# A scan kernel on one core: the residual add of each unit moves from VectorE to TensorE and ScalarE, and unit 0 and the end are reordered

## The reference

```python
h = table_slice[x]                                   # a gather, (2, 2048, 64)
# mixer on layernorm(h):
r = x_in = layernorm(h)
proj = layernorm(x_in, g, b) @ in_w.T                # -> conv input, gate
act = silu(dwconv(conv_input))
for way in (forward, backward):                      # mamba: conv, silu, dt, B, C
    state = state * exp(dt * A) + (dt * u) * B       # scan over 2048 tokens, 128 channels x 16 states
    y = sum_n(state * C) + u * D
    out_way = (y * silu(z)) @ out_w_way.T
h = h + (concat(fwd, bwd) * silu(gate)) @ out_w.T + r
# then a top-1 mixture of 32 small experts on layernorm(h), added to h
```

## Time and profile before

| what | value |
|---|---|
| median of 3 runs | 562.32 us (561.82 to 569.52) |
| the profiled execution's own time | 559.91 us |
| its span in the profile | 558.1 us |
| DVE busy | 489.1 us (88%) |
| POOL busy | 474.9 us (85%) |
| PE busy | 457.3 us (82%) |
| ACT busy | 372.6 us (67%) |
| chain that ended last, by engine | DVE 45%, PE 24%, issue 11%, ACT 9%, POOL 6% |

### The profile page before, as it was taken

One profiled execution on the slowest core, in us unless ns is written; L12 is line 12 of the kernel. 1 busy time (PEld: TensorE's weight loads), 2 busy tenths in 40 slices (PEclk: granted clock), 3 DMA queues, 4 the chain that ended last, 5 costly groups with the idle time before them and its releaser, 6 DMA issues.

```text
span 558.1 us, 5617 instructions
## 1 busy us (share of the span) xinstructions
PE 457.3 (82%) x1621; PEld 175.5 (31%) x1621; DVE 489.1 (88%) x606; ACT 372.6 (67%) x651; POOL 474.9 (85%) x157
## 2 busy tenths in 40 slices
PE   2976977868889797979798889888988895785877
PEld 1422422313233231424232423232324232332243
DVE  3575895989899999999999899999998999999940
ACT  2488485686877776776968497869684974564433
POOL 5552877998989989899999999999999999989700
PEclk9998998999989897989999799999997997697998
DMA  4249397949293855738493949493939392900000
GB/s 58 18 63 218 77 218 149 217 114 207 76 199 88 182 124 134 173 87 175 115 181 117 200 115 190 119 197 105 201 109 208 98 208 86 222 13 1 5 5 19
DMA packets 51008, 71.05 MB, mean 127 GB/s; under 512 B 16498, under 2 KB 17442, under 8 KB 50978
## 3 DMA queue, kind: packets, MB, share of 16 engines
q1 hardware_dynamic: 47986, 69.36, 55.0%
q0 software_dynamic: 1024, 1.05, 2.4%
q10 hardware_dynamic: 1968, 0.29, 0.3%
HBM read 60.19 MB, written 10.49 MB: 127 GB/s over the span
## 4 chain that ended last, share of the span: by engine, by line
DVE 45%; PE 24%; issue 11%; ACT 9%; POOL 6%; DMA 3%; SPq 2%; POOLq 0%; DVEq 0%; ACTq 0%
DVE st L1504 26%; DVE st L1489 8%; POOL st L491 4%; PE ps L727 3%; ACT ps L1081 2%; PE ps L628 2%; PE ps L690 2%; PE ps L703 2%; PE ps L817 2%; PE ps L715 2%; DVE zr L1510 1%; PE ps L801 1%; ACT L979 1%; PE ps L698 1%; DVE ga L1516 1%
## 5 line engine op out<-in xcount | busy, mean ns | idle before, releaser
L491 POOL TENSOR_TENSOR st<-st,repC 128x2048 f32<-128x2048 f32 x63 | 285.2, 4530 | 18.1 <-ACT carry L1087 13.0
L1504 DVE TENSOR_TENSOR_SCAN st<-ps,carry,st 128x512 f32<-128x512 f32 x192 | 235.5, 1268 | 3.7 <-ACT ps L1081 3.1
L1081 ACT ACTIVATE ps<-dtS,negA 128x512 f32<-128x512 f32 x256 | 171.2, 682 | 63.1 <-DVE st L1504 61.8
L482 POOL TENSOR_TENSOR st<-duS,repB 128x2048 f32<-128x2048 f32 x30 | 135.9, 4530 | 1.7 <-issue 1.7
L1504 DVE TENSOR_TENSOR_SCAN st<-ps,zero,st 128x512 f32<-128x512 f32 x64 | 78.9, 1270 | 1.4 <-ACT ps L1081 1.0
L715 PE MATMUL ps<-st,fold 128*32 128x512 f32 x504 | 69.0, 620 | 12.8 <-POOL st L491 12.8
L1489 DVE TENSOR_TENSOR st<-duS,ps 128x2048 f32<-128x2048 f32 x33 | 75.0, 2272 | 1.9 <-PE ps L690 1.7
L628 PE MATMUL ps<-act,wT 128*128 128x512 f32 x128 | 57.8, 593 | 0.3 <-ACT act L1025 0.3
L463 POOL DMA_INDIRECT x<-in_L_tok_ple_table,idx x32 | 31.1, 973 | 29.6 <-DMA dtS<-dt_dram 13.4
L690 PE MATMUL ps<-xr,Bw 128*128 128x512 f32 x68 | 38.2, 645 | 6.2 <-ACT bc_sb L1073 6.2
L667 PE MATMUL ps<-xr,wT 128*32 128x512 f32 x32 | 18.1, 649 | 26.3 <-DVE st L1489 26.3
(11 more groups left out here) (138 smaller groups left out, 622.2 us busy)
## 6 DMA issues: line engine op xcount, KB each, us to landing
repC<-bc_dram SPq DMA_DIRECT2D x64, 256.0 KB, 10.5
duS<-du_dram SPq DMA_DIRECT2D x60, 256.0 KB, 4.7
dtS<-dt_dram SPq DMA_DIRECT2D x60, 256.0 KB, 7.8
repB<-bc_dram SPq DMA_DIRECT2D x60, 128.0 KB, 2.9
dt_dram<-dt SPq DMA_DIRECT2D x16, 256.0 KB, 3.0
du_dram<-du SPq DMA_DIRECT2D x16, 256.0 KB, 2.0
bc_dram<-bc_sb SPq DMA_DIRECT2D x16, 64.0 KB, 11.1
dtS<-dt_dram SPq DMA_DIRECT2D x8, 128.0 KB, 3.4
```

The costliest lines, as they stand in the source:

```text
L482: pool.tensor_tensor(st[:, r], duS[:, u % 2], row, ALU.mult).then_inc(sem("dbu_pool"), 1)
L491: pool.tensor_tensor(st[:, r], st[:, r], row, ALU.mult).then_inc(sem("hc_ready"), 1)
L1081: sc.activation(decay_bank(u, r, q), dtS[:, u % 2, q], ACT.Exp, scale=negA[:, way(u), q, r:r + 1]).then_inc(sem("decay_ready"), 1)
L1504: dve.tensor_tensor_scan(st[:, r, q, order], decay_bank(u, r, q)[:, order], st[:, r, q, order], first, ALU.mult, ALU.add).then_inc(sem("sc ...
```

## The change

It has five parts.

1. For units 0 to 14 `partial` first multiplies the identity by `x0` (256 columns, start) and then adds its four products, so that PSUM holds the new h. A new `new_x` on ScalarE, at p = 10 of the next unit, copies it back to `x0` and increments `x0_added`. `add_partial` of these units leaves VectorE's p = 7. Unit 15 keeps `add_partial`.
2. VectorE's two copies of constants (L1661, L1662) move from p = 4 of unit 0 to before the first scan.
3. In unit 0 GpSimd runs `dt_times_x(1)` ahead of `by_c(0, 0)`, the last four gathers behind `by_c(0, 2)`, and `dt_times_x(2)` in unit 1 behind `by_c(0, 3)`. SyncE issues `load_B(1)` ahead of `store_dt(1)`. ScalarE's `dt_out(u)` also waits for `du_ready`.
4. TensorE runs `turn_chunk(3)` behind `skip_product(0)` and `add_nought(3)`.
5. At the end TensorE runs `logits(before)` ahead of the third of the last four `sum_states` products, all four `hidden(before, k)` ahead of `turn_normed(last)`, and one new `add_nought` ahead of `logits(last)`. ScalarE's order follows. VectorE runs `by_gate(last)` ahead of `choice(before)`.

```diff
             store_bc(1)
+            load_B(1)
             store_dt(1)
             store_du(1)
             load_du(1)
-            load_B(1)
...
+                if u == 1:
+                    dt_times_x(2)
                 if u == 0:
                     pool.wait_ge(sem("dt_first_1"), 64)
                     for t in range(TB + 4, TB + 12):
                         gather(t)
+                    dt_times_x(1)
                 if 2 in on_pool(u):
                     input_product(u, 2)
                 by_c(u, 0)
-                if u == 0:
-                    dt_times_x(1)
-                    for t in range(TB + 12, TILES):
-                        gather(t)
                 by_c(u, 1)
                 if u + 1 < UNITS:
                     input_product(u + 1, 0)
                 by_c(u, 2)
-                if u + 2 < UNITS:
+                if u == 0:
+                    for t in range(TB + 12, TILES):
+                        gather(t)
+                if 0 < u < UNITS - 2:
                     dt_times_x(u + 2)
...
+                if u + 1 < UNITS:
+
+                    pe.wait_ge(sem("u_added"), CB * batch(u) + (CB if way(u) else chunk(u) + 1))
+                    if way(u):
+                        pe.wait_ge(sem("x0_added"), u)
+                    pe.matmul(ps[:, SHORT, 0:TC * DM], ident[:], x0_of(tile0(u)).rearrange("p t d -> p (t d)"),
+                              start=True, stop=False, skip_group_check=True)
                 for t in range(TC):
                     mm = pe.matmul(ps[:, SHORT, t * DM:t * DM + DM], ga[:, t * P:t * P + P],
-                                   wT[:, 14, DM * way(u):DM * way(u) + DM], start=True, stop=True)
+                                   wT[:, 14, DM * way(u):DM * way(u) + DM], start=(u + 1 == UNITS), stop=True,
+                                   skip_group_check=True)
...
-            turn_chunk(3)
             skip_product(0)
             add_nought(3)
+            turn_chunk(3)
...
             for q in range(NQ):
+                if q == 2:
+                    logits(before)
                 if q < NQ - 1:
                     pe.wait_ge(sem("hc_ready"), NR * UNITS + q)
                 else:
-                    logits(before)
                     pe.wait_ge(sem("hc_dve"), 1)
...
             hidden(before, 2)
+            hidden(before, 3)
             turn_normed(last)
-            hidden(before, 3)
+            add_nought(1, start=True)
             logits(last)
...
             def dt_out(u):
                 sc.wait_ge(sem("dt_ps"), u)
                 wait(sc, "dt_in_dram", 16 * u)
+                sc.wait_ge(sem("du_ready"), u)
...
+            def new_x(u):
+
+                sc.wait_ge(sem("attn_ps"), u + 1)
+                sc.activation(x0_of(tile0(u)), ps[:, SHORT, 0:TC * DM].rearrange("p (t d) -> p t d", d=DM), ACT.Copy) \
+                  .then_inc(sem("x0_added"), 1)
...
                 if p == 10:
+                    if is_unit(u - 1):
+                        new_x(u - 1)
...
             hidden_relu(before, 2)
+            hidden_relu(before, 3)
             normed_out(last)
-            hidden_relu(before, 3)
...
             rates(1)
+            dve.wait_ge(sem("consts"), 1)
+            ch.mark(dve.tensor_copy(rank[:], ranki[:]))
+            ch.mark(dve.tensor_copy(w1[DM:DM + E], maskf))
+            ch.wait()
...
                 if p == 7:
-                    if is_unit(u - 1):
-                        add_partial(u - 1)
...
             first_best()
+            by_gate(last)
             choice(before)
-            by_gate(last)
             add_partial(last)
```

More of the change, by code:

```diff
@@ L1658, in first_unit @@
                     input_product(0, 1)
[L1659 to L1663, removed]
                 if p == 5:
```

## The result

The changed kernel takes 553.38 us (median of 4 runs, 552.02 to 555.21) against 562.07 us (4 runs). The ratio is 0.9878, 95% interval 0.9843 to 0.9913. That is 1.2% less, a gain clear of noise but smaller than 2%. The forecast was 554.0 us in a range of 549.0 to 561.5. The profiled execution took 554.74 us with a span of 552.9, 5.2 us less than the profiled one of before. The medians lie 8.7 us apart; the ratio makes it 6.9 us.

What follows compares the result with a forecast made beforehand. VectorE was taken to set the pace from 96 to 259 and 484 to 529 us, GpSimd between. Gains 1.6 + 2.5 - 0.6 + 2.3 + 2.5 = 8.3 us against the median 562.32 gave 554.0 us, range 549.0 to 561.5.

Steps and rivals of the forecast that it cites:

- Unit 0: Work moved into waits lets TensorE's chain from `sum_dt(1)` start earlier: 2.3 us gained, between 1.0 and 3.5.
- The clock step: At `sum_dt(1)` in unit 0, TensorE's clock falling to half for 2 to 5 us would lose 1.0 to 2.5 us.
- The other reorderings: GpSimd's and SyncE's new orders in units 0 and 1 hide; uncovered, SyncE's loads would cost 0.6 us.
- Units 1 to 5: VectorE sets the pace, so each removed residual add gains 0.32 us: 1.6 us gained.
- Rival C: TensorE becomes the bound, delaying convolution, table load and decays 15 and 0: 5.5 us lost, 567.8 us; chance 0.06.
- Units 6 to 11: GpSimd is full, so removed adds gain nothing; late `partial` costs 0.3 us in units 8 and 12: 0.6 lost.
- rival A: TensorE falls to 1.2 GHz at `sum_dt(1)` and the end: 4.4 us gained, 557.9 us; chance 0.24 together with D.
- Units 12 to 15: VectorE's adds and waits for `partial` go near the last units: 2.5 us gained, between 1.45 and 3.7.
- The end: Reordered last products 1.5 us gained, `by_gate` swap 0.6 lost, full clock in `experts_out(before)` 1.6 gained: 2.5 us.
- the second sum_states pair: At the end, with `logits(before)` moved ahead, the last two `sum_states` products run together: 1.5 us gained.
- The swap of `by_gate`: At the end, `by_gate(last)` ahead of `choice(before)` makes TensorE's `turn_choice(before)` wait: 0.6 us lost.
- Rival D: ScalarE's wait for `partial` replaces VectorE's and decays come late, part 1 worth nothing: 557.5 us; 0.24 together with A.

Runs made afterwards that it cites:

- all_parts: The changed kernel once more, timed beside its parts on the same chip against the kernel before: ratio 0.9896, median 553.38 us.
- end_no_zero: The changed kernel without its one zero product ahead of `logits(last)`: ratio 0.9931 to the kernel before, median 556.27 us.
- end_only: The kernel before with the changes of the end alone (part 5): ratio 0.9976 to the kernel before, median 558.53 us.
- moved: The changed kernel with no zero product ahead of `sum_states(u, 0)`, two ahead of `sum_states(u - 1, 2)`, ScalarE's copy at p = 9: ratio 0.9894 to before, 555.23 us.

## Why the prediction was right, and where it was not

The time (554.0 against 553.4) and the sign were right. The terms can be measured as differences to the one profile of before, in the changed kernel's first profile and in its second (all_parts), in us gained:

| term | forecast | first profile | second profile |
|---|---|---|---|
| unit 0, up to by_gate in unit 1 | 2.3 | 3.77 | 3.16 |
| units 1 to 5 | 1.6 | 0.36 | -0.53 |
| units 6 to 11, up to by_gate in unit 12 | -0.6 | -3.49 | 0.15 |
| from there to VectorE's last product | 2.5 | 1.97 | 1.96 |
| the end, up to the last fin | 2.5 | 2.53 | 2.54 |
| sum | 8.3 | 5.1 | 7.3 |

- **Unit 0**, taken as 2.3 between 1.0 and 3.5. The copies cost nothing, VectorE no longer waits for `b_rows(0, 1)`, and the chain from `sum_dt(1)` moved by 59.94 - 56.37 = 3.57 us in the first profile, the upper end. That a TensorE chain and not VectorE's 4.8 us sets the size is shown by the new 1.67 us wait, which stands in all eleven profiles (1.66 or 1.67 us). The clock step was right as well: in three of them the clock falls at `sum_dt(1)` and 1.6 us are lost, inside the 1.0 to 2.5 allowed. In four more the chain is late because the clock was low ahead of unit 0, a case that the prediction did not have. The other reorderings hid as forecast: GpSimd's `dt_times_x(2)` waits for nothing now.
- **Units 1 to 5**, taken as 1.6: 0.4 and -0.5 measured. The step that failed is the one that gave every add 0.32 us of VectorE's pace there. Rival C's mechanism, TensorE's longer `partial` passed on through the convolution to the table load, was already at work there. In unit 1 it takes 0.32 us, as the doubled product shows, and unit 2 gets 0.2 us longer. I had granted it to units 8 and 12 alone and had put the slack of decay 15 at 0.8 us. The product is also dearer than its 0.45 us (0.54).
- **Units 6 to 11**, taken as 0.6 lost with GpSimd never idle. From 255 to 475 us GpSimd is busy for 216.53 of 220.0 us in the first profile, and 3.5 us are lost. In the second it is busy for 219.35, and nothing is lost, close to the forecast. The difference is the low clock at the places shown, which is rival A's mechanism at another place than rival A had it.
- **Units 12 to 15**, taken as 2.5 between 1.45 and 3.7: 2.0 in both profiles, in the lower half.
- **The end**, 2.5: the second sum_states pair gained 1.2 (from VectorE's product of the last block to `y_by_z`: 532.14 - 528.77 = 3.37 before, 528.32 - 526.16 = 2.16 after; forecast 1.5). The swap of `by_gate` lost 0.27 (4.35 against 4.08 from `y_by_z` to the add; forecast 0.6). The clock gained 1.6 as forecast. The first two terms were both a little too large and cancel. end_no_zero shows that the zero product is the cause of the third; no row of before had shown that a zero product pays.
- **Rival D** is out. With part 1 undone the kernel tends to be slower, and the copy mostly hides: it waits 2.8 us in all fifteen units, 1.75 of them in unit 8. **Rival C's time** did not come, though its mechanism did in small. Its sum took 0.9 us a unit at half clock for units 6 to 14 but 0.45 for units 1 to 5; with 0.9 in all of them it would have been 570.1 us.
- **The Trainium skill's rule** that an add with one SBUF input does not block GpSimd stood: `by_c` takes 4.53 us in both kernels. The prediction gave the rule of "SBUF — State Buffer", section "Who interferes with whom", without the exception stated there, the two-port performance modes, which copies and casts can enter. The add cannot; the cast in the last section waited as such an operation would.

Part of the close hit is luck. The measured terms add up to 5.1 and 7.3 us in the two profiles, the ratios give 6.9 and 5.8 us, and only the medians of the first measurement gave 8.7. That base, 562.32, was high as well: beside the experiments the kernel before had medians of 560.2 to 560.8. The sum claimed too much in units 1 to 5, and unit 0 made up for a part of it. How the gain divides over many executions is not settled, since the parts' own ratios have intervals of 0.3 to 0.7% to either side.

## What to carry to other kernels

Where two engines are both near full, a step taken from one is worth its time only if the engine that now does it has room at that point of the unit: follow the new work down its queue to the next waiting instruction, in every stretch, and look at more than one profile. A zero product costs its time where others wait for TensorE. Where TensorE waits for someone else anyway it can earn more than it costs: at the end of this kernel it did (1.6 us), in the middle it raised the mean clock, but two changes that each seemed to help did not help together. Filling an idle gap with work that was due later, as in unit 0, brought scan 12 forward in all eleven profiles, by 0.8 to 4.1 us, but the clock decided how much of it, and not all of it reached the end.

## What the hardware showed that I had not expected

- The same cast of 128x32 integers took 2.67 us beside a GpSimd product and 0.18 us where GpSimd waited. It had ended with GpSimd's `dt_times_x` (at 66.3). In end_only, where the cast stands at its old place, it took 1.45 us and ended with `by_c` at 65.1; the small copy behind it then took 1.44 us instead of 0.42. The Trainium skill, "SBUF — State Buffer", section "Who interferes with whom", has casts and copies among the operations that can block on the port pair shared with GpSimd for the whole of the other's instruction; these durations agree with it. Part 2 thus saved 2.5 us of work too, and did not only hide it.
- One kernel's executions differ by 4.6 us (551.34 to 555.90 in all_parts) with the same instructions. In the two profiles of the changed kernel the difference lies where TensorE's granted clock is 1.2 GHz for 3 to 7 us: from 268 to 278 and from 304 to 314 us the mean clock is 0.66 in the slower one and 0.83 in the faster, and units 6 and 8 take 29.3 and 30.4 us against 27.5 and 28.0. In moved, unit 9 takes 2.9 us more than before (31.03 against 28.09), with the low clock on the row of B and the convolution that ScalarE's table load waits for.
